# The first scores of attention behind the row maxima of five steps, and three steps' worth of maxima per step after them

## What is computed

```python
scores = jnp.einsum('bhqd,bhkd->bhqk', q, k) / math.sqrt(HEAD_DIM)
causal = jnp.tril(jnp.ones((seq_len, seq_len), dtype=bool))
scores = jnp.where(causal[None, None, :, :], scores, jnp.float32(-1e+20))
attn = jax.nn.softmax(scores, axis=-1)
out = jnp.einsum('bhqk,bhkd->bhqd', attn, v)
```

## Time and profile before

| quantity | us |
| --- | --- |
| median of 3 runs | 3591.53 |
| lowest and highest run | 3586.33 and 3592.12 |
| profiled execution | 3592.34 |
| its span, first to last instruction | 3590.5 |
| attention, first maximum to last scores | 690.3 to 2750.7 |
| opening of attention, first maximum to first scores | 690.31 to 723.48 |

### The profile page before, as it was taken

The page is one execution under the profiler, slowest core; times in us unless marked ns, Lnnn a source line. Parts: engine busy times, 40 slices in busy tenths (PEclk is TensorE's granted clock), DMA queues, the critical chain, the costliest instruction groups (busy, mean ns, idle before and its releaser), DMA issues. The chain is left out here.

```text
span 3590.5 us, 62180 instructions
## 1 busy us (share of the span) xinstructions
PE 3407.1 (95%) x25088; PEld 2360.7 (66%) x25088; DVE 2269.7 (63%) x3912; ACT 1413.4 (39%) x1660; POOL 2236.0 (62%) x1029
## 2 busy tenths in 40 slices
PE   1999999899999999999999999999996699999999
PEld 1778888656666666666666666666663388888887
DVE  3577776677777677777767777776770444444443
ACT  2222232145555555555555555555554210011110
POOL 4443220068989998998999899899887022222222
PEclk8999999789999999999999999999998699999999
DMA  9999873412122112212212221221111533334432
GB/s 234 246 249 233 234 208 115 121 35 50 38 62 53 41 48 58 51 38 62 53 41 49 58 51 37 63 54 40 49 31 52 181 72 92 93 93 93 93 93 65
DMA packets 245886, 325.90 MB, mean 91 GB/s; under 512 B 64090, under 2 KB 153818, under 8 KB 245634
## 3 DMA queue, kind: packets, MB, share of 16 engines
q1 hardware_dynamic: 227202, 255.29, 26.5%
q0 software_dynamic: 18432, 67.12, 8.8%
HBM read 223.74 MB, written 97.52 MB: 89 GB/s over the span
## 5 line engine op out<-in xcount | busy, mean ns | idle before, releaser
L742 DVE TENSOR_REDUCE mpart<-mx_ps 128x1 f32<-128x512 f32 (+3 forms) x2560 | 1432.7, 605 | 519.3 <-PE mx_ps L795 338.5
L711 ACT ACTIVATE probs<-st_ps 128x1024 f32<-128x1024 f32 (+1 forms) x1152 | 1063.8, 974 | 852.3 <-PE st_ps L826 621.1
L792 PE MATMUL mx_ps<-k_max,qs 96*128 96x512 f32 (+3 forms) x2560 | 908.5, 416 | 19.9 <-POOL masks L660 17.0
L826 PE MATMUL st_ps<-qs,k_score 98*128 98x512 f32 (+1 forms) x2304 | 723.2, 408 | 0.2
L685 POOL TENSOR_TENSOR sums<-probs 128x1024 f32<-128x1024 f32 x256 | 609.5, 2381 | 161.4 <-ACT probs L711 161.3
L792 PEld LDWEIGHTS mx_ps<-k_max,qs 96*128 96x128 f32 x2560 | 467.7, 195 | 297.1 <-DVE mpart L742 188.9
L687 POOL TENSOR_TENSOR sums<-sums,probs 128x1024 f32<-128x1024 f32 x256 | 608.8, 2378 | 25.5 <-ACT probs L711 6.9
L844 PE MATMUL od_ps<-probs,vs 128*32 128x256 f32 (+1 forms) x9216 | 592.1, 375 | 0.0
L693 POOL TENSOR_TENSOR sums<-sums,probs 128x1024 f32<-128x1024 f32 (+1 forms) x256 | 538.7, 2104 | 20.4 <-ACT probs L711 0.4
L826 PEld LDWEIGHTS st_ps<-qs,k_score 98*128 98x128 f32 x2304 | 421.3, 194 | 72.5 <-ACT probs L711 11.9
L1058 POOL TENSOR_TENSOR h<-h,bb 128x1024 f32<-128x1024 f32 x32 | 105.1, 3283 | 542.8 <-DVE xn_c L1156 542.8
(11 more groups left out here) (104 smaller groups left out, 4006.2 us busy)
## 6 DMA issues: line engine op xcount, KB each, us to landing
qs<-q_hi_scratch SPq DMA_DIRECT2D x128, 256.0 KB, 4.6
h_scratch<-hbuf SPq DMA_DIRECT2D x32, 512.0 KB, 8.4
q_hi_scratch<-rot_hi SPq DMA_DIRECT2D x64, 256.0 KB, 3.5
q_lo_scratch<-rot_lo SPq DMA_DIRECT2D x64, 256.0 KB, 4.2
qs<-q_lo_scratch SPq DMA_DIRECT2D x64, 256.0 KB, 5.7
o_scratch<-od_sb SPq DMA_DIRECT2D x128, 128.0 KB
o_in<-o_scratch SPq DMA_DIRECT2D x32, 512.0 KB, 4.5
o_in<-recip_scratch SPq DMA_DIRECT2D x128, 128.0 KB, 7.7
```

The lines of the kernel that those rows point to most:

```text
L711: nc.scalar.activation(probs[:, n % SLOTS, half, :, lo:QW], st_ps[:, half, :, lo:QW], ACT.Exp, scale=float(HD) ** -0.5).then_inc(exp_done, 1)
L742: nc.vector.tensor_reduce(mpart[:, h * TPC + t, kc:kc + 1], mx_ps[:, e % MAX_BANKS, 0:w], AX, ALU.max).then_inc(max_done, 1)
L792: mm = nc.tensor.matmul(out, qs[c][0:K_ROWS, h, t * P:(t + 1) * P], k_max[0:K_ROWS, kc * CT:kc * CT + w], start=True, stop=not diagonal)
L826: mm = nc.tensor.matmul(out[:, :, lo:QW], k_score[0:M_ROW + 2, kt * P:(kt + 1) * P], qs[c // 2][0:M_ROW + 2, h:h + 2, at + lo:at + QW], st ...
```

## The change

`FIRST_LEAD` becomes 5, and the lead of the first group grows by three steps' worths per step instead of one and a third:

```diff
@@ -468,7 +468,7 @@
 SETS = sum_sets()
 SET_OF = [j for j, steps in enumerate(SETS) for s in steps]
-LEAD, FIRST_LEAD = 18, 12
+LEAD, FIRST_LEAD = 18, 5
 TURN_AFTER = 5
@@ -495,7 +495,7 @@
-    lead = lambda k: min(FIRST_LEAD + k + k // 3, k + LEAD) if first else k + LEAD
+    lead = lambda k: min(FIRST_LEAD + 3 * k, k + LEAD) if first else k + LEAD
```

## The result

The changed kernel is slower: median 3598.01 us of 22 runs (3595.51 to 3603.66) against 3592.26 us for the kernel before on the same chips. Two of the 22 runs of the kernel before, 5100.71 and 5874.85 us, were slow ones and are left out of the ratio. The medians are 5.8 us apart; the ratio, 1.0019 with a 95% interval of 1.0012 to 1.0025, gives +6.8 us, from +4.3 to +9.0. I forecast 3594.5 us, +3.0 us, range 3586 to 3602. The profiled execution took 3602.54 us with a span of 3600.6 us, 10.1 us more than before. That difference of one execution against one is not all the change's. The first row maximum starts at 694.52 us against 690.31 before (4.2 us), and across the twelve other kernels of this study, whose work before attention is the same, that start lay between 686.3 and 692.9 us.

The account below looks back on a forecast made before the run. VectorE was taken to bound the opening, TensorE the steady part. First scores at 706.9 us plus 63.5, 0.7 and 37.2 us gave 808.3 against 805.28, +3.0 us: median 3594.5 us, range 3586 to 3602.

Parts of the forecast that it names:

- Term 1: End of the first group's opening: first scores start at 706.9 us, 16.6 us earlier, after a short wait for row sends.
- Term 2: Steps 0 to 6 of the first group, packed with more maxima: 63.5 us, with the clock alternating.
- low walk: Step-by-step count of steps 0 to 6 with TensorE's clock low throughout: 69.1 us.
- high walk: Step-by-step count of steps 0 to 6 with TensorE's clock high from the middle of step 3: 58.0 us.
- rival C: Low clock holds through steps 0 to 6: +8.6 to +13 us, 3600 to 3604 us; chance 0.18.
- Term 3: Steps 7 to 17 of the first group, with 46 entries as in later groups: 37.2 us against 49.2 before.
- A: The earlier start of the exponentials counts in full: 16.6 us faster, 3574.9 us; chance 0.05.
- B: Clock rises early and stays up: -7.5 to -2.5 us, 3584 to 3589 us; chance 0.12.
- D: Key loads or row sends hold the first scores longer: over +13 us if the delay exceeds 10 us; chance 0.05.

Follow-up runs that it names:

- spread kernel: Against the changed kernel, same short opening but the catching up spread to about 7 entries in steps 3 to 17; ratio 1.0002.
- late doubling: The changed kernel with each maximum's matmul issued twice, for entries 24 to 117 alone; ratio 1.0006.
- batch split: The changed kernel with each step's last maximum moved into the batch, between the products of the two key halves; ratio 1.0468.

## Why the prediction held, point by point

**Term 1 held.** The first scores were forecast 2 us behind the last maximum, with a wait of some 2 us and VectorE dry for 3: 2.16 and 3.38 us. From the first reduce they start at 15.96 us (711.12 - 695.16), forecast 15.94 (706.9 - 690.96).

**Term 2 held in size**, in part by luck. From the scores of step 0 to those of step 7: forecast 63.5 us, measured 775.68 - 711.12 = 64.6 us. The 63.5 was the mean of two walks, 58.0 and 69.1, and not worked out from a course of the clock. By the first exponentials steps 0 to 6 took 9.4, 9.6, 9.5, 11.1, 6.5, 11.7 and 5.7 us. Step 0 took 1.4 us more than either walk had; step 3 went as in the low walk, steps 4 and 6 nearly as in the high one. The clock rose later than the high walk assumed, at 751 us, at the end of step 3. Its mean from 707 to 770 us is 0.59, just under the 0.6 at which rival C was to decide. But this trace's stage starts 4.2 us later than in the kernel before; in the window moved by as much, 711.2 to 774.2 us, the mean is 0.63, inside the 0.6 to 0.85 that I named, at its low end. VectorE had gaps of up to 2.2 us behind its dry spell at the first scores, where I had written "nearly without gaps".

My use of the Trainium skill there ("TensorE: Matmul & The Clock Gate", section "A second HAM failure mode: psum-queue depth-cycling") went too far: it tells of a clock that goes up and down, and 69.1 us is the walk with the clock low throughout. The stretches at 0.50, 0.84, 0.63 and 1.00 of this trace agree with the up and down.

**Term 3 held.** 37.2 us forecast and measured.

**The sum** was +3.0 us; the trace's distance says +4.1, and the 1.1 us between them are term 2's. The timed +6.8 us (4.3 to 9.0) does not take in the +3.0, though the median of 3598.01 us lies in the range that I gave. It is 2.7 us above the trace's distance; 1.0 us of that stands behind step 18. One trace holds one course of the clock, and what the rest is stays open.

**The rivals.** A, the whole lead counting (-16.6 us), and B, an early rise of the clock, did not come. C, the clock low through steps 0 to 6, did not come in full: it was low through steps 0 to 3. D did not come either: the rows came when forecast.

**What the working had wrong** is its reading of the packed steps. I wrote that what the earlier scores win is lost in steps 0 to 6. In the sum that is so, but it suggests that spreading the maxima would keep the gain, and I then expected 100 to 107 us from that; the trace gave 117.5. The comparison that was missing is what an entry costs in each place: the 33 moved ones cost 0.50 us each in the opening (0.56 if the new wait of 2.2 us is left out) and 0.63 us in steps 0 to 3, so they cost about as much wherever they go. What remains is what the new place adds: the row wait (3.1 us with what follows from it, read from the kernel with four maxima moved) and the clock (2.9 us or more, read from the kernel that keeps it up). Together they exceed the 4.1 us, and with both away the kernel is level with the one before. I also put no price of its own on the row wait in the rivals, and it is as large as the clock's.

How strong is this? Each cause was taken away by itself and both together, and the traces moved as they should. But each trace is one execution, and the timed ratios can't tell the two causes apart (1.0009 and 1.0006, with intervals that overlap the changed kernel's). The ratio of the spread kernel, 1.0002, is the one that does not fit.

## What to carry to other kernels

Before work is moved from one phase to another to start a third engine earlier, price it at its scarcest engine in both places. Here a maximum cost about 0.6 us of VectorE in either, and a start 16.4 us earlier was worth nothing as it was, and at most some 1 to 3 us with its new losses taken away. An earlier start brings out waits that lay hidden behind the work moved. Keep as much independent work between a send and its reader as the send takes (here 5.2 us from the transpose at 705.87 us to the scores at 711.12 us, which eight maxima covered and four did not). And look at how far ahead the steady state runs: two steps less of lead gave 7.5 us, where no kernel with another opening or ramp was faster than the one before.

## What the runs showed of the hardware

TensorE was counted busy for all of the 30 us from 715 to 745 us of the changed kernel, and the granted clock stayed at 0.50. Part of this was pacing by VectorE: nine maxima from 731.69 us took 5.42 us, 0.60 us each, where one takes 0.43 us at that clock. But from 715 to 728 us masked maxima and scores followed one another without a gap, and the clock stayed down as well. A second matmul for each maximum raised the clock to 0.97 between the first scores and step 7, and the distance was 2.9 us shorter. In the kernels with 4 to 10 maxima a step the same doubling made the distance 1.6 and 2.9 us longer.

One more interleaving of 32-column products with full-width matmuls cost about 0.3 us at the high level, 156 us in all over 576 batches.

The two sends of the negated maxima reached their reader 5.1 to 6.0 us behind the start of the transpose in the four traces in which TensorE waited for them (5.1 with the late doubling, 5.2 in the changed kernel, 5.7 with the batch split in it, 6.0 in the spread one).
